# Reordering the stages of a linear-attention unit and of the first token group in a fused attention + MoE layer on one Trainium2 core

## The reference

```python
q, k, v = silu(xn @ Wq), silu(xn @ Wk), silu(xn @ Wv)          # 16 heads of 32
# per head, in chunks of 128 tokens, state S [32, 32], decay ld < 0:
scores = (q_c @ k_c.T) * D                                     # D: causal mask times exp(ld * distance)
o_c    = scores @ v_c + (q_c @ S) * exp(ld * (i + 1))
S      = exp(128 * ld) * S + (k_c * exp(ld * (127 - i))).T @ v_c
o      = o * sigmoid((xn @ Wg1) @ Wg2)                         # gate, then an RMS norm per head, times norm_w
attn   = o @ Wo
# moe: softmax(xn @ Wg) over 8 experts, the best 2 of each token, capacity 640 per expert
moe    = sum over the 2 of  gate * (relu(xn @ w1[e]) @ w2[e])  # w1 [8, 512, 2048], w2 [8, 2048, 512]
```

## Time and profile before

| | |
|---|---|
| time, median of 3 runs | 2024.02 us (2022.81 to 2024.14) |
| profiled execution | 2022.43 us, its span (first to last instruction) 2020.7 us |
| busy over the span | PE 99%, PEld 81%, DVE 45%, ACT 27%, POOL 36% |
| chain of work that ended last | PE 98%, ACT 1% |
| granted TensorE clock | 0.998 of full speed over the span, 0.83 from 10 to 20 us |
| attention | to about 543 us, the experts behind it |
| DVE busy, 140 to 180 us | 29.14 of 40 us |

### The profile page before, as it was taken

The page is one execution under the profiler, slowest core; times in us unless marked ns, Lnnn a source line. Parts: engine busy times, 40 slices in busy tenths (PEclk is TensorE's granted clock), DMA queues, the critical chain, the costliest instruction groups (busy, mean ns, idle before and its releaser), DMA issues.

```text
span 2020.7 us, 29044 instructions
## 1 busy us (share of the span) xinstructions
PE 1997.1 (99%) x11720; PEld 1638.8 (81%) x11720; DVE 899.5 (45%) x1792; ACT 550.6 (27%) x986; POOL 723.7 (36%) x600
## 2 busy tenths in 40 slices
PE   7999999999999999999999999999999999999998
PEld 6788777878788888888888888888888888888886
DVE  7777777767752234234323422522252234324311
ACT  6322232223232133123212312421232123123211
POOL 5555544545442324324332431432142314233211
PEclk9999999999999999999999999999999999999999
DMA  7012121212351234214233431521162125224121
GB/s 238 30 64 85 34 75 64 85 40 69 127 153 27 47 60 140 44 56 122 64 65 77 124 45 50 142 57 28 47 159 41 35 47 160 37 63 104 37 32 21
DMA packets 85506, 151.45 MB, mean 75 GB/s; under 512 B 18304, under 2 KB 18304, under 8 KB 85360
## 3 DMA queue, kind: packets, MB, share of 16 engines
q1 hardware_dynamic: 61312, 105.64, 16.3%
q0 software_dynamic: 24048, 43.76, 12.8%
HBM read 109.82 MB, written 39.53 MB: 74 GB/s over the span
## 4 chain that ended last, share of the span: by engine, by line
PE 98%; ACT 1%; issue 0%; POOL 0%; DVE 0%; DMA 0%; POOLq 0%; ACTq 0%
PE bank L1232 49%; PE bank L1499 34%; PE bank L1363 4%; PE bank L1239 2%; PE bank L1554 2%; PE bank L1286 2%; PE bank L1352 1%; PE bank L1346 1%; PE bank L1260 1%; PE bank L1329 1%; PE bank L1320 0%; PE bank L1374 0%; ACT intra_decay L679 0%; DMA ld_row<-in_L_attn_log_decay 0%; PE bank L1295 0%
## 5 line engine op out<-in xcount | busy, mean ns | idle before, releaser
L1179 DVE SCALAR_TENSOR_TENSOR h_lo<-bank,h_hi 128x512 fp32r<-128x512 f32 x254 | 175.2, 690 | 745.5 <-ACT h_hi L826 745.2
L618 POOL DMA_INDIRECT gathered<-xn_rows,gather_row x304 | 320.2, 1053 | 474.3 <-DVE x_blocks L1045 292.5
L1232 PE MATMUL bank<-xT_hi,w_hi 128*128 128x512 f32 x1024 | 398.8, 389 | 0.0
L1232 PE MATMUL bank<-xT_hi,w_lo 128*128 128x512 f32 x1024 | 398.6, 389 | 0.0
L1232 PE MATMUL bank<-xT_lo,w_hi 128*128 128x512 f32 x1024 | 398.6, 389 | 0.0
L1499 PE MATMUL bank<-w_hi,h_hi 128*128 128x512 f32 x1016 | 395.4, 389 | 0.0
L1499 PE MATMUL bank<-w_lo,h_hi 128*128 128x512 f32 x1016 | 395.4, 389 | 0.0
L1499 PE MATMUL bank<-w_hi,h_lo 128*128 128x512 f32 x1016 | 395.4, 389 | 0.0
L826 ACT ACTIVATE h_hi<-bank 128x512 fp32r<-128x512 f32 x254 | 151.7, 597 | 797.3 <-PE bank L1232 797.2
L631 POOL DMA_INDIRECT out_rows<-y,add_row x80 | 128.8, 1611 | 546.9 <-ACT y L819 473.1
L1232 PEld LDWEIGHTS bank<-xT_hi,w_hi 128*128 128x128 f32 x1024 | 192.2, 188 | 40.4 <-issue 0.9
(11 more groups left out here) (203 smaller groups left out, 2302.4 us busy)
## 6 DMA issues: line engine op xcount, KB each, us to landing
raw_weights<-in_L_ffn_w SPq DMA_DIRECT2D x256, 256.0 KB, 11.6
x_in<-in_L_attn_x SPq DMA_DIRECT2D x32, 256.0 KB, 3.6
xn_rows<-xn SPq DMA_DIRECT2D x32, 256.0 KB, 2.5
x_res<-in_L_attn_x SPq DMA_DIRECT2D x32, 256.0 KB, 4.9
out_rows<-y_attn SPq DMA_DIRECT2D x28, 256.0 KB, 2.0
gathered<-xn_rows,gather_row POOLq DMA_INDIRECT x304, 3.7
out_rows<-y,add_row POOLq DMA_INDIRECT x80, 5.3
attn_raw<-in_L_attn_Wq SPq DMA_DIRECT2D x4, 256.0 KB, 5.3
```

Of the source, the lines that this page charges most:

```text
L618: pool.indirect_dma_start(xg[:, nth % 2, q * P:(q + 1) * P], None, xn_pieces, bass.IndirectOffsetOnAxis(ap=gather_row[:, col, q:q + 1], ax ...
L1179: v_.scalar_tensor_tensor(lo[:, 0:n * P], h_bank[f % 2][:, 0:n * P], 0.0, hi[:, 0:n * P].bitcast(F32), ALU.max, ALU.subtract).then_inc(S[" ...
L1232: last = mm(dest, at(left[l], t), at_r(right[r], t), start=(i == 0), stop=(i == n - 1))
```

## The change

In a unit, PE now does `score(u)`, `project_gate(u)`, `project("k", u+1)`, `project("q", u+1)`, `turn_kd(u+1)`, `attend(u)`, `update_states(u+1)`. So k comes ahead of q, the next unit's keys are turned ahead of the attend, and the states' update follows it; only in the first unit of a group does the update stand behind the score. The gate goes into q's bank. In i = 3 the small product comes ahead of `turn_kd`, the logits are turned behind the attend into `t_bank`, and `count` stands behind all four v products. ACT, POOL and DVE are reordered to go with it: ACT takes k's silu before q's and copies the turned keys ahead of `oT_high`; POOL spreads a group's 8 scatters as 2, 3 and 3 over two units; DVE does `gate_low` ahead of the gated output. For the first group, high parts of q's weights are made ahead of the tokens', q's first pass is done between the transposes of the tokens, the small and v products get banks of their own, and the decay tables of heads 8 to 15 are made after the first unit's tanh. For u = 30, ACT's four casts of expert weights move from between the two silus to behind the copy of the keys.

```diff
-        xn_bank = [sc[0], sc[1], proj[0], proj[1]]
+        first_xn_bank, first_small_bank, first_v_bank, xn_bank = sc, sc[0], sc[1:], [sc[0], sc[1], proj[1], proj[0]]
...
                 if i == 0:
                     pool.wait_ge(S["scored"], u + 1)
-                    for t, r in ROUTES[:ahead]:
+                    for t, r in ROUTES[:2]:
                         route(g, t, r)
-                if u > 0 and i > 0:
-                    head_scales(u - 1)
                 if u < ATTN_UNITS - 1:
                     decayed_k(u + 1)
-                    if u > 0 and i == 0:
+                    if i < 2:
+                        for t, r in ROUTES[2 + 3 * i:5 + 3 * i]:
+                            route(g, t, r)
+                    if u > 0:
                         head_scales(u - 1)
                     decayed_q(u + 1)
...
                 if u > 0:
                     square(u - 1)
                 if u < ATTN_UNITS - 1:
+                    silu_k(u + 1)
                     silu_q(u + 1)
-                    if u == ATTN_UNITS - 2:
-                        for n in range(FPC, UNITS):
-                            split_high(0, n)
-                    silu_k(u + 1)
                 if i == 2 and g < SUPERS - 1:
                     for j in range(TPG):
                         xnT_high(TPG * (g + 1) + j)
+                if i == GROUPS - 1 and g < SUPERS - 1:
+                    copy_logits(g + 1)
+                if u < ATTN_UNITS - 1:
+                    copy_kd(u + 1)
+                if u == ATTN_UNITS - 2:
+                    for n in range(FPC, UNITS):
+                        split_high(0, n)
                 if 1 < u < ATTN_UNITS - 1:
                     oT_high(u - 2)
...
+            turn_xn(0, lambda j: first_q_high(j - 2) if j > 1 else None)
+            for j in range(TPG - 2, TPG):
+                first_q_high(j)
...
             for u in range(ATTN_UNITS - 1):
                 g, i = u // GROUPS, u % GROUPS
                 score(u)
-                turn_kd(u)
                 if i == 0:
+                    update_states(u)
                     pe.wait_ge(S["g1_lo_made"], g + 1)
...
                 project_gate(u)
-                pe.wait_ge(S["q_ready"], u + 1)
-                if i == 0:
-                    pe.wait_ge(S["v_ready"], TPG * (g + 1))
+                pe.wait_ge(S["k_ready"], u + 1)
+                if i == 2:
+                    wait(pe, ("y_ready", TPG * g))
+                project("k", u + 1, proj[1], "k_projected")
+                pe.wait_ge(S["tanh_ready"], u + 1)
                 project("q", u + 1, proj[0], "q_projected")
-                update_states(u)
-                pe.wait_ge(S["tanh_ready"], u + 1)
-                project("k", u + 1, proj[1], "k_projected")
...
+                if i == GROUPS - 1:
+                    pe.wait_ge(S["k_ready"], u + 2)
+                    project_small(g + 1)
+                turn_kd(u + 1)
                 attend(u)
+                if i < GROUPS - 1:
+                    update_states(u + 1)
...
                     project_v(TPG * (g + 1) + 2)
-                    count(g + 1)
                     pe.wait_ge(S["v_ready"], TPG * (g + 1) + 2)
                     project_v(TPG * (g + 1) + 3)
+                    count(g + 1)
```

159 lines of the change are left out of this document (97 added, 62 removed).

## The result

The changed kernel takes 2030.3 us (median of 8 runs, 2029.0 to 2031.8), the kernel before 2023.6 us beside it (8 runs, 2022.8 to 2024.3): ratio 1.0034, 95% interval 1.0025 to 1.0043. It is **slower**, by 6.7 us, where the prediction had 2023.1 us, no change that can be told, and a range that ended at 2027.9. The profiled execution took 2030.2 us with a span of 2028.4.

The account below looks back on a forecast made before the run. PE, busy 99% of the span, was taken to bound the kernel. Terms -6.0 - 1.3 + 0.8 + 4.2 + 1.4 + 0 = -0.9 from the median 2024.0 gave 2023.1 us, range 2017.0 to 2027.9.

Parts of the forecast that it names:

- Part F: First group: earlier q pass partly fills the 2.8 us wait, masks and scatter stay; 0, bounds -2.8 and +1.5.
- Part A: Update follows attend: joints between kinds of matmul go, 0.19 us each in 24 units, less elsewhere; -6.0 us.
- Part B: Unit 2: PE's wait for kdT goes, the keys' decay now being ahead of scatters and head scales; -1.3 us.
- Part C: Ordinary units: kdT on POOL stalls DVE's states, so attend waits 0.2 us in 7 units (i = 1); +0.8 us.
- Part D: First unit of 6 groups: late count delays masks; scale_heads and kdT tie, DVE taken first; 0.7 each, +4.2 us.
- rival 1: States are not held up by kdT; Part C is 0 and Part D 1.8: 2019.8 us, chance 0.15.
- attend is now due at S + 7.33: Ordinary unit, S being its score's start: attend, which needs DVE's states, due at S + 7.33, before S + 7.91.
- Part E: Unit 30: four ACT casts of expert weights delay masks that PE waits for; +1.4 us, bounds 0 and 2.2.
- rival 2: First group passes its gain on: 2.8 us wait filled, first attend not held; 2020.3 us, chance 0.13.
- rival 3: First units of groups: POOL's kdT ahead of DVE's scale_heads, 6 x 0.8 us more; 2027.9 us, chance 0.12.
- rival 4: Ordinary units: kdT late for turn_kd, 0.36 us in 24 units, 8.7 us; 2031.8 us, chance 0.06.
- rival 5: POOL's head scales hold DVE up: masks 0.35 to 0.9 late, 18 units pay 0.4; 2030 us, chance 0.04.

Follow-up runs that it names:

- run 1: Changed kernel with decay tables 8 to 15 made ahead of the first silu: 2027.6 us, ratio 1.0019 to the kernel before.
- run 2: Changed kernel with the first q pass whole, four 512-column matmuls after the four tokens' turns: 2026.2 us, ratio 1.0016 to the kernel before.
- run 8: Changed kernel with the edits of run 1, run 2, run 3 and run 6 together: 2015.3 us, ratio 0.9961 to the kernel before.
- run 4: Changed kernel with the update back between gate and k in units not first in a group: 2033.1 us, ratio 1.0045 to the kernel before.
- run 18: Run 15 with the update between gate and k (edit of run 4), on a fourth chip: 2018.0 us, ratio 0.9977 to the kernel before.
- run 7: Changed kernel with only the routing count back ahead of each group's last v product: 2026.1 us, ratio 1.0014 to the kernel before.
- run 3: Changed kernel with DVE's states ahead of the mean square and head scales: 2020.9 us, ratio 0.9987 to the kernel before.
- run 5: Kernel before with DVE's states ahead of the mean square and head scales, as in run 3: 2022.7 us, ratio 0.9998.
- run 6: Changed kernel with unit 30's weight casts and unit 29's first_rows made later: 2026.7 us, ratio 1.0015 to the kernel before.
- run 17: Run 15 again on a fourth chip, without issue gaps: 2012.7 us, ratio 0.9948 to the kernel before.
- run 15: Run 8 with the prologue rearranged and unit 1's keys ahead of the scatters on POOL, on a third chip: 2037.8 us, ratio 0.9889 to the kernel before.

## Why the prediction was wrong

**Part F failed, by 5 us.** I gave the first group 0, with a bound of +1.5; it costs 5.0 by unit 1's score. Two terms were missing. The first is in unit 0, which takes 3.8 us longer. I saw that the tables move ahead of the keys' silu and charged their time to POOL's slack, but not the two function changes of 1.28 us that moving Exp between tanh and silu brings, nor the wait of 2.25 us for the keys, nor the granted clock of 0.50 behind it; run 1 takes these away and starts unit 1's score 2.6 us earlier. The second stands ahead of unit 0, whose score starts 1.2 us late. I let the first q pass be a gain because it starts earlier, without pricing sixteen matmuls of 128 columns against four of 512; with the pass whole, unit 1's score starts 3.1 us earlier (run 2). How much of that is the number of matmuls and how much the pace is open. The two gains do not add: with both edits (run 8) it is 2.7 us.

**Parts A to D were near in sum, and by luck.** For groups 1 to 6 their terms make about +0.4 us (0.19 x 18 + 0.085 x 6 + 0.1 x 6 gained, +0.7 and +4.2 paid); measured +1.1. But the waits for states in these 24 units are 8.0 us where C and D have 4.9, and what the order gains beside them is 6.9 us where A has 4.5: two misses that nearly cancel. Part A's joint costs 0.22 to 0.31 where I had 0.19 (runs 4, 18), and at 0.31 that is most of its miss. Part B is right: units 1 to 3 give back 2.3 us, 1.3 of it that wait. Part D's 0.7 for each first unit is 0.7 a group in run 7, which takes away the late count alone. The tie of D came out both ways: POOL first in odd groups, a wait of 1.46 as worked out (1.5), DVE first in even ones, 0.85 for 0.7. C's mechanism, that DVE stands still in `kdT`, is in the rows of unit 4 for `scale_heads` and in run 3 for a state (0.98). In the changed kernel 23 of the 80 `state` rows are longer than 0.35 us, mostly 0.40 to 0.67 and not the 0.9 that I looked for; rival 1 fell. But one step of C and D was false: "attend is now due at S + 7.33". The states are due at the turn, 0.42 earlier, since the turn writes the bank they are read from; the line `wait(pe, ("states_ready", u))` in `turn_kd` is unchanged, but called one unit earlier it asks for the states of the running unit. Waits of 9.2 us in 12 units stand against the 5.0 of C and D. That the states' place is what costs is shown by runs 3 and 5 together; that it is due to these 0.42 us is not shown.

**Part E was too small, by about 2 us.** The wait for the masks near 530 us is 1.5 as forecast (1 to 2), but the end of the attention costs 3.2 us, where E's 1.4 less the joints' gain gives about 1. Of the rest, 1.2 us is in unit 29, where scatters moved one unit later on POOL reach DVE through a DMA; run 6 takes away 1.1 us there and 0.9 of the wait for the masks. I had followed the scatters past POOL's own work only.

**Rivals.** 2 is refuted (first masks at 38.87, not ahead of 37.9); 3 is half true (POOL first, but in odd groups only); 4 is false, `kdT` was late for a turn only in unit 0; 5 is false: `oT_lo` is never stretched beyond 0.79, and 33 state and carry operations that lie wholly inside a `head_scale` of POOL take their 0.35 us. So the rule of the Trainium skill ("SBUF — State Buffer", on shared ports), that a VectorE instruction with two SBUF inputs and a GpSimd instruction that reads SBUF exclude each other, holds in these traces for `kdT` (0.98 for a state, 1.54 for `scale_heads`) and not for `head_scale`. The slow side came true through none of the rivals, but mainly through the prologue.

## What to carry to other kernels

Price a moved block of code by what changes at its two new neighbours: here an activation function of another table cost a load of 1.28 us on both sides, and what was put ahead of an engine's other work made all of that late. When an operation that writes a buffer moves ahead of its last user, the buffer's producer becomes due earlier; look for the wait in the moved function, not in the place it left. And a reorder of one engine wants the same reorder in its partners: with DVE's states moved to match, the same change is a gain of 2.8 us (run 3), and with the prologue and the end mended too one of 10.8 us (run 17).

## What the hardware showed that I had not expected

**On two of the four chips of runs 1 to 18 TensorE stood idle between short matmuls, and on the one of them where the changed kernel ran, the sign of this change was another.** The kernel before takes 2061 and 2066 us on the two instead of 2023. No run went back to one of these chips later, so it is not shown that this belongs to the chip and not to a state that it was in. The update behind the attend in unit 0 in the same kernel, first on the chip with 2038 us (run 15), then on the one with 2013 us (run 17):

```profile
42.44 0.60 PE L1367 MATMUL bank<-v,kd 128*32 128x32 f32 x11
43.49 0.25 PE L1367 MATMUL bank<-v,kd 128*32 128x32 f32 x4 [0.45 <-issue]
44.21 0.29 PE L1367 MATMUL bank<-v,kd 128*32 128x32 f32 x5 [0.47 <-issue]
44.97 0.28 PE L1367 MATMUL bank<-v,kd 128*32 128x32 f32 x4 [0.47 <-issue]
45.70 0.28 PE L1367 MATMUL bank<-v,kd 128*32 128x32 f32 x6 [0.45 <-issue]
47.12 0.23 PE L1367 MATMUL bank<-v,kd 128*32 128x32 f32 x2 [1.15 <-issue]
```

```profile
42.45 0.48 PE L1367 MATMUL bank<-v,kd 128*32 128x32 f32 x32
42.85 1.17 PE L1322 MATMUL bank<-qT,kT 32*128 32x128 f32 x32
```

(The trace has two rows for each of these matmuls of the program, 32 for 16.) The profile shows nothing that PE waits for; four to six rows run, then PE idles 0.45 us, and the update takes 4.9 us instead of 0.4. Unit 0 is the worst: in the later units with i = 0 and i = 1 the update behind the attend has two such gaps, with i = 2 none. Behind the five of unit 0 the granted clock of the window 48 to 50 us is 0.50 (1.00 without gaps at 44 to 46), and the score takes 2.0 us instead of 1.1. In the whole attention it is 24.7 us (unit 31's score at 539.26 against 514.61), and the experts behind it, with their long matmuls, lose nothing (1495.6 us against 1496.2). All of this loss is in one stage. From the first row of an update to the row behind it, summed from unit 1's score to unit 31's, the updates take 32.7 us instead of 10.8 in this kernel and 23.1 instead of 10.7 in the changed one; the scores take 34.0 and 33.1 instead of 33.2. The list of waits has less than that, because the rows between the gaps are slower too: 16.3 us of gaps in this kernel and, in the changed one,

```profile
PE bank L1364 <- issue: 6.2, 15, 0.5
```

The gaps of the changed kernel too are in units with i = 0 and i = 1, in the update behind the attend. None is behind a wait of 1.46 us for a state, while one or two are behind waits of 0.36 and 0.85 us and where PE did not wait (unit 0, behind its 2.25 us, has a short one of 0.26).

With the update between two products the changed kernel has 1.5 us of such gaps, all at the scores (which then take 38.4 us instead of 33.1). There run 4's edit is 2.2 us less by the medians, with intervals that overlap, and not 2.7 more. From 43.49 to 45.70 us 13 rows were started, one in 0.17 us. The Trainium skill ("TensorE: Matmul & The Clock Gate", on the issue floor) knows a mode of the sequencer that spends 62 ns on a matmul; no run here shows which mode a chip is in. That instructions arrive too slowly is the reading that fits, but it was not tested; why it is so on two chips is open. So is where the kernel before loses its 38 us, because no trace of it was taken on such a chip: that its attend, score and turn stand in one row is only an argument. What the runs do show is that the same comparison of these two kernels gave 1.0034 in one place and 0.9911 in another.

**The pace at the start of the program.** In the changed kernel eight 512-column matmuls of 16.9 to 20.4 us took 0.44 us each at a granted clock of 1.00 in the windows; in run 2 the same ones took 0.23, also at 1.00. The short matmuls ahead of them are not needed for it: in run 8, where the pass is whole and PE had idled 3.0 us, the matmuls of 15.6 to 20.8 us took 0.42 to 0.46 each, again at 1.00. In the kernel before, after an idle 2.8 us, they took 0.43 from 15.6 to 19.0 us, and there the granted clock is 0.50 in the window 16 to 18. In run 2 PE had idled 0.8 us. So the slow pace is the one that the kernel before had at the 1.2 GHz level, though in the two others the windows show 1.00; why it came in the changed kernel, where PE's only wait between its first transpose and these rows was 0.5 us, no run tells.
